# Edge preparation: two of the three weighted key one-hots are multiplied on GpSimd instead of VectorE

## The chip, the cores and the metric

The kernel runs on one core of one Trainium2 chip. The metric is device time of a whole execution in microseconds; the kernel before has a median of 10035.09 us over 3 runs (10032.35 to 10036.63). A core has TensorE (matrix multiply, writes PSUM), VectorE, ScalarE, GpSimd and SyncE (which here only issues DMAs). In rows of the profile they are PE (PEld is its weight load), DVE, ACT, POOL and SP.

## What is computed

Four graph layers run one after the other over 6250 nodes with 128 features and 200,000 edges sorted by target node: a GCN, a typed message layer with a GRU, an attention layer and an MPNN, each added to its input and normalized.

```
x = _layernorm(x + _L0_gnn_ref(x, edge_index, edge_weight, W, b))
x = _layernorm(x + _L1_gnn_ref(x, edge_index, edge_type_8, ...))
x = _layernorm(x + _L2_gnn_ref(x, edge_index, ...))
x = _layernorm(x + _L3_gnn_ref(x, edge_index, edge_attr_64, ...))
```

Each layer gathers a row per edge (by `src`) and sums rows per target (by `dst`). The GCN weighs an edge by `edge_weight`. All layers share the same edges, so the kernel sorts the edges into a table once, before the first layer. That preparation is the part changed here.

## The kernel before

Edges come in 112 groups of 14 x 128 (GC = 14 columns on 128 partitions). An *item* is one group against one window of 128 target nodes; there are 112 items here, handled by a loop of 28 turns with four items each (SL = 4). Every engine runs its own loop over the same items, and semaphores keep them in step.

For an item k the work is this; lines are those of the profile.

- GpSimd *picks*: it copies and shifts the item's slices of the edge fields into small tiles (L681 to L691), among them `w2`, the edge weight split into three bf16 parts, each value doubled. It starts once TensorE has finished the window sums (L958) of item k - 2, since `product` counts those, and signals `posted`.
- VectorE, `key_hot(k)`: the window test and the key (L778, L779), then OJ, the one-hot of each edge's key, 128 x 1372 bf16 (1372 = 14 x 98; L783), and how many edges of the same row have the same key (L785 to L789).
- TensorE, `ranks(k)` (L934 to L939): prefix sums and totals of OJ into PSUM.
- VectorE, `rank_hot(k - 1)`, in the turn after: copies of the prefix sums from PSUM (L804, L805), the product of OJ and the prefix (L808), three folding steps (L810 to L812), an add (L813), the one-hot of the rank OHr (L814) and a maximum (L817).
- ScalarE: two of the five fields of OJF, OJ times a per-edge number (L719), and copies of the edge terms out of PSUM (L708).
- VectorE, `weigh_keys(k)`: the other three fields of OJF, OJ times each part of `w2` (L839, three instructions of 128 x 1372 bf16).
- TensorE, `place(k)` (L949), one turn later: 14 matmuls that place the five fields by OHr; it waits for OHr (`hot_rank`), ScalarE's fields (`scaled`) and VectorE's (`wdone`).
- VectorE, `rec_add(k - 2)`: what was placed is added from PSUM into X and acc (L827, L830).
- VectorE, `window_hot(k)` (L846), and TensorE's window sums from it (L958). TensorE also multiplies the edge attributes in the loop (L969).

So one turn on VectorE is `key_hot(k)`, `rank_hot(k-1)`, `rec_add(k-2)`, `weigh_keys(k)`, `window_hot(k)`, and one on TensorE is half of the edge terms, `ranks(k)`, `place(k-1)`, the other half, window sums of k. OJ, OJF and w2 have two buffers each, by the parity of the item; OJF is 128 x 14 x 5 x 98, so one field of it is 14 pieces of 98 elements that lie 490 apart. Most VectorE instructions wait on the one before through the semaphore `chain` (the helper `own.step`).

Two other places of the program are used below to read prices: the GCN pass, where GpSimd adds the three parts of the weights (L1651, L1653, 128 x 2450) while VectorE subtracts tiles (L1675, 128 x 896 f32).

Of the kernel before, what the change touches and what calls it, by code (L numbers as in the profile page):

```python
# [30 lines left out]
ALU = mybir.AluOpType  # L31
# [17 lines left out]
SL = 4  # L49
# [20 lines left out]
BK = 2 * NT  # L70
# [37 lines left out]
def passed(eng, tick):  # L108

    eng.sem_inc(tick, 1)

def over(ap, n):

    return ap.unsqueeze(2).to_broadcast([ap.shape[0], ap.shape[1], n])
# [7 lines left out]
def build(nc, x, xT, src, dst, edge_type, edge_weight, edge_attr, wpack, mats, rowpack, colpack, out):  # L124
    V = nc.vector
# [37 lines left out]
    def sems(prefix, names):  # L163

        made = [nc.alloc_semaphore(name=f"{prefix}_{n}") for n in names.split()]
        in_stage.extend(made)
        return made
# [8 lines left out]
    with ExitStack() as whole:  # L176
# [372 lines left out]
        with ExitStack() as ctx:  # L549
# [8 lines left out]
            w2 = sb(ctx, "prep_w2", [P, 2, 3, GC, 2], BF16)  # L558
# [12 lines left out]
            OJ = sb(ctx, "prep_OJ", [P, 2, GC, BK], BF16)  # L571
            OJF = sb(ctx, "prep_OJF", [P, 2, GC, 5, BK], BF16)
# [24 lines left out]
            zeroed, posted, hotd, hot_key, scaled, wdone, prefix_ready, prefix_free, hot_rank, place_ready, place_free = sems(  # L597
                "prep", "zeroed posted hotd hot_key scaled wdone prefix_ready prefix_free hot_rank place_ready place_free")
# [2 lines left out]
            totalled, slots_out, begun, taken = sems("prep", "totalled slots_out begun taken")  # L601
            fields_blank, ends_out, cleaned = sems("prep", "fields_blank ends_out cleaned")
            attr_in = sems("prep", "attr_in0 attr_in1")
            terms_out = sems("prep", "terms_out0 terms_out1")
            term_ready, term_taken, terms_done, spares, si_ready = sems("prep", "term_ready term_taken terms_done spares si_ready")
            KEY_STEPS, RANK_STEPS, ADD_STEPS = 6, 8, 2
            STEPS = KEY_STEPS + RANK_STEPS + ADD_STEPS
            with nc.Block() as block:
# [55 lines left out]
                @block.gpsimd  # L664
                def _(pool):
                    nc.gpsimd.memset(OJF[:], 0.0).then_inc(fields_blank, 1)
                    pool.wait_ge(zeroed, 1)
                    n = pool.value_load(turns_to[0:1, NCH:NCH + 1], min_val=1, max_val=KCAP // SL)
                    with pool.Fori(0, n) as i:
                        for s in range(SL):  # L670
                            k, par = i * SL + s, s % 2
                            pool.wait_ge(item_ready[s], i * 16 + 16)
                            passed(pool, tick)
                            g = pool.value_load(itm[0:1, s, 2:3], min_val=0, max_val=NG - 1)
                            pool.wait_ge(hot_key, k + 1)
                            pool.wait_ge(scaled, k + 1)
                            pool.wait_ge(wdone, k + 1)
                            pool.wait_ge(product, k + 1)
                            pool.wait_ge(hotd, k + 1)
                            fg = FLD[:, ds(g, 1)].rearrange("p g f c -> p (g f) c")  # L680
                            nc.gpsimd.tensor_copy(dg[:], dstI[:, ds(g * GC, GC)])  # L681
                            nc.gpsimd.tensor_copy(kg[:], KEY0[:, ds(g * GC, GC)]).then_inc(taken, 1)
                            pool.wait_ge(taken, k + 1)
                            passed(pool, tick)
                            nc.gpsimd.tensor_scalar(off[:, par], dg[:], itm[:, s, 0:1], None, ALU.subtract)
                            nc.gpsimd.tensor_scalar(kk[:, par], kg[:], itm[:, s, 3:4], None, ALU.subtract)
                            nc.gpsimd.tensor_scalar(at[:, par], over(dg[:], 2), itm[:, s, 0:1], None, ALU.subtract)
                            nc.gpsimd.tensor_copy(fld[:, par], fg[:, 0:2, :])
                            nc.gpsimd.tensor_copy(w2[:, par].rearrange("p f c a -> p (f c) a"),
                                                  over(FLD[:, ds(g, 1), 2:5, :].rearrange("p g f c -> p (g f c)"), 2))  # L690
                            nc.gpsimd.tensor_copy(wm[:, par, 0:3], fg[:, 2:5, :]).then_inc(posted, 1)  # L691
                            pool.wait_ge(posted, k + 1)
                            passed(pool, tick)
                    pool.wait_ge(terms_done, 1)
                    pool.iota(spare_rows, [[P, NG * GC]], base=NSLOT, channel_multiplier=1,
                              allow_small_or_imprecise_dtypes=True).then_inc(spares, 1)
# [42 lines left out]
                def _(dve):  # L739
                    own = Chain(dve, begun)  # L740
# [4 lines left out]
                    own.step(V.memset(RK[:], 0.0))  # L745
                    own.step(V.memset(within[:], 0.0))
                    own.step(V.memset(wm[:], 1.0))
                    own.step(V.tensor_copy(iob[:], iota_row[:]))
                    own.step(V.tensor_tensor(out=lower[:], in0=over(iota_row[:, 0:GC], GC), in1=rows(iota_row[:, 0:GC], GC),
                                             op=ALU.is_gt))  # L750
# [6 lines left out]
                    dve.sem_inc(hot_key, 2)  # L757
                    dve.sem_inc(scaled, 2)
                    dve.sem_inc(wdone, 2)
                    dve.sem_inc(hotd, 2)  # L760
                    dve.sem_inc(place_free, 1)
                    dve.wait_ge(fields_blank, 1)

                    def pairs(a2, n):
                        return a2.unsqueeze(2).to_broadcast([P, GC, n // 2, 2])

                    def halves(t):
                        return t.rearrange("p c (h a) -> p c h a", a=2)

                    def same_rows(b, n):  # L770
                        return b.rearrange("p (h a) -> p h a", a=2).unsqueeze(1).to_broadcast([P, GC, n // 2, 2])

                    def key_hot(k, s, own):
                        par = s % 2
                        n0 = own.n
                        dve.wait_ge(posted, k + 1)
                        dve.wait_ge(hot_key, k + 2)
                        own.step(V.tensor_single_scalar(win[:], off[:, par], 7, op=ALU.arith_shift_right))  # L778
                        own.step(V.scalar_tensor_tensor(out=key2[:], in0=over(win[:], 2), scalar=MISS, in1=over(kk[:, par], 2),  # L779
                                                        op0=ALU.mult, op1=ALU.add))  # L780
                        dve.wait_ge(scaled, k + 1)
                        dve.wait_ge(wdone, k + 1)
                        V.tensor_tensor(out=halves(OJ[:, par]), in0=pairs(key2[:], BK), in1=same_rows(iob[:, 0:BK], BK),  # L783
                                        op=ALU.is_equal).then_inc(hot_key, 1)
                        own.step(V.tensor_tensor(out=twin[:], in0=over(key2[:, :, 0], GC), in1=rows(key2[:, :, 0], GC),  # L785
                                                 op=ALU.is_equal))
                        own.step(V.tensor_tensor(out=twin[:], in0=twin[:], in1=lower[:], op=ALU.mult))
                        own.step(V.tensor_reduce(within[:, par], twin[:], AX, ALU.add))
                        own.step(V.scalar_tensor_tensor(out=within[:, par], in0=win[:], scalar=0.0, in1=within[:, par],  # L789
                                                        op0=ALU.is_equal, op1=ALU.mult))  # L790
                        assert own.n - n0 == KEY_STEPS
# [42 lines left out]
                    def weigh_keys(k, s):  # L834
                        par = s % 2
                        dve.wait_ge(hot_key, k + 3)
                        dve.wait_ge(place_ready, k + 1)
                        for a in range(3):
                            ins = V.tensor_tensor(out=halves(OJF[:, par, :, 2 + a, :]), in0=halves(OJ[:, par]),  # L839
                                                  in1=pairs(w2[:, par, a], BK), op=ALU.mult)  # L840
                        ins.then_inc(wdone, 1)

                    def window_hot(k, s):
                        par = s % 2
# [5 lines left out]
                    with dve.Fori(0, n) as i:  # L850
# [3 lines left out]
                        for s in range(SL):  # L854
                            k = i * SL + s
# [69 lines left out]
                def _(pe):  # L925
# [16 lines left out]
                    def place(k, s):  # L942
                        par = s % 2
                        pe.wait_ge(hot_rank, k + 2)
                        pe.wait_ge(scaled, k + 3)
                        pe.wait_ge(wdone, k + 3)
                        pe.wait_ge(place_free, k + 2)
                        for c in range(GC):
                            mm = pe.matmul(placed[par], OHr[:, par, c, :], OJF[:, par, c].rearrange("p f b -> p (f b)"),  # L949
                                           start=c == 0, stop=c == GC - 1)  # L950
                        mm.then_inc(place_ready, 1)
# [2274 lines left out]
```

## Time and profile before

| | |
|---|---|
| median of 3 runs | 10035.09 us |
| the profiled execution | 10033.66 us, span 10031.9 us |
| busy, TensorE matmul / VectorE / ScalarE / GpSimd | 8345.2 / 7403.1 / 3377.0 / 2329.2 us |
| mean granted TensorE clock | 0.883 of full speed |
| edge loop of preparation | about 123 to 1545 us, 14% of the span |
| granted clock in the loop | 0.91 |

The span runs from the first to the last instruction. Shares of busy time over the whole span mix stages with different limits, so the loop is looked at by itself, from the first to the last of the weight multiplies. Two instructions whose times overlap by a few hundredths are pipelined on one engine. An instruction's time in the profile includes any time for which it was issued and could not proceed.

### The profile page before, as it was taken

The numbers are of one execution on the slowest core, as the hardware profiler recorded it, in microseconds if no ns is written. First come the engines' busy times: TensorE is split into PE (matmuls) and PEld (weight loads), VectorE is DVE, ScalarE is ACT, GpSimd is POOL, SyncE is SP. The second block draws the span as 40 slices with busy tenths as digits, with TensorE's granted clock in tenths as the row PEclk, the third lists the DMA queues.
The fourth block names the chain that finished last, engine by engine and source line by source line (L and its number), as shares of the span: only waits on it lengthen the run. The fifth ranks groups of instructions, "written<-read, shape, count | busy, mean of one in ns | idle before, by whom it ended". The sixth has DMA issues, their size and how long they took to land. (4 is left out here: it accounts for less than half of the span.)

```text
span 10031.9 us, 275228 instructions
## 1 busy us (share of the span) xinstructions
PE 8345.2 (83%) x104317; PEld 6699.0 (67%) x104318; DVE 7403.1 (74%) x11896; ACT 3377.0 (34%) x7132; POOL 2329.2 (23%) x3048
## 2 busy tenths in 40 slices
PE   5777772599959999996699999955886999599983
PEld 4545551599946666664466666635886999499982
DVE  7888888888857666664466766635997888788875
ACT  4777771100015444443244444411330000133321
POOL 2111110000014555553155555510331000100010
PEclk8999995799969999998799999976557999699986
DMA  3333331566633333331233333302772222166650
GB/s 97 110 110 110 110 110 43 164 248 248 248 137 132 115 122 118 121 116 60 68 119 119 121 115 122 114 30 80 302 294 88 94 93 92 66 247 248 248 190 11
DMA packets 393197, 1349.67 MB, mean 135 GB/s; under 512 B 111251, under 2 KB 174781, under 8 KB 354621
## 3 DMA queue, kind: packets, MB, share of 16 engines
q1 hardware_dynamic: 261629, 1054.90, 29.5%
q10 hardware_dynamic: 72704, 173.74, 4.6%
q0 software_dynamic: 58688, 118.70, 3.8%
q8 instruction: 109, 1.79, 0.1%
q14 instruction: 67, 0.55, 0.0%
HBM read 940.84 MB, written 406.28 MB: 134 GB/s over the span
## 5 line engine op out<-in xcount | busy, mean ns | idle before, releaser
L2077 PE MATMUL typed_GP<-typed_hd,typed_Gb 128*128 128x256 bf16 x15288 | 1942.5, 274 | 0.0
L2012 ACT CAST typed_Gb<-typed_GP 128x768 bf16<-128x768 f32 (+1 forms) x1568 | 1336.5, 852 | 1276.0 <-PE typed_GP L2058 635.6
L2077 PEld LDWEIGHTS typed_GP<-typed_hd,typed_Gb 128*128 128x128 bf16 x15288 | 1366.9, 98 | 555.2 <-issue 250.9
L1919 POOL DMA_INDIRECT es_d<-X x1568 | 1574.9, 1004 | 525.1 <-issue 476.7
L1964 DVE TENSOR_TENSOR typed_hd<-typed_recv,typed_iota2b 128x768 bf16<-128x768 bf16 (+1 forms) x1568 | 929.6, 593 | 642.2 <-PE typed_GP L2077 642.0
L1974 DVE CAST typed_Gb<-typed_GP 128x384 bf16<-128x384 f32 (+1 forms) x1568 | 925.1, 590 | 322.5 <-PE typed_GP L2062 166.5
L2058 PE MATMUL typed_GP<-typed_H,typed_hsT 128*32 128x384 bf16 x18816 | 1054.8, 330 | 66.7 <-ACT typed_H L2005 66.7
L719 ACT ACTIVATE prep_OJF<-prep_OJ,prep_fld 128x98 bf16<-128x98 bf16 x3136 | 861.9, 368 | 123.3 <-DVE prep_OJ L783 123.1
L2058 PEld LDWEIGHTS typed_GP<-typed_H,typed_hsT 128*32 128x32 bf16 x18816 | 357.6, 95 | 523.6 <-issue 237.9
L949 PE MATMUL prep_PS<-prep_OJF,prep_OHr 128*128 128x490 bf16 x1582 | 466.7, 461 | 234.2 <-DVE prep_OHr L814 234.2
L1806 PE MATMUL mpnn_GP<-mpnn_hd,mpnn_et 128*128 128x128 f32 x4802 | 578.7, 277 | 2.4 <-issue 1.4
L1806 PE MATMUL gcn_GP<-gcn_hd,gcn_msg 128*128 128x128 f32 x4802 | 578.6, 277 | 0.0
L1806 PE MATMUL heads_GP<-heads_hd,heads_msg 128*128 128x128 f32 x4802 | 578.5, 277 | 0.0
L1806 PEld LDWEIGHTS mpnn_GP<-mpnn_hd,mpnn_et 128*128 128x128 f32 x4802 | 551.6, 192 | 2.7 <-issue 2.7
L1806 PEld LDWEIGHTS gcn_GP<-gcn_hd,gcn_msg 128*128 128x128 f32 x4802 | 551.7, 192 | 0.0
L1806 PEld LDWEIGHTS heads_GP<-heads_hd,heads_msg 128*128 128x128 f32 x4802 | 551.6, 192 | 0.0
L1758 ACT ACTIVATE mpnn_et<-mpnn_et 128x1536 f32<-128x1536 f32 x196 | 296.1, 1511 | 646.9 <-DVE mpnn_et L1709 646.9
L1958 DVE TENSOR_SCALAR typed_hsT<-typed_rows,iota_col 128x384 bf16<-128x384 bf16 (+1 forms) x1568 | 508.6, 324 | 0.0
L949 PEld LDWEIGHTS prep_PS<-prep_OJF,prep_OHr 128*128 128x128 bf16 x1582 | 175.3, 116 | 482.4 <-issue 217.4
L1791 PE MATMUL gcn_GP<-gcn_H,gcn_hsT 128*128 128x128 bf16 x7203 | 437.2, 220 | 37.0 <-ACT gcn_H L1750 27.6
L1693 DVE TENSOR_TENSOR mpnn_hd<-recD,iota 128x1536 f32<-128x1536 f32 (+1 forms) x196 | 351.1, 1792 | 154.8 <-PE mpnn_GP L1806 154.8
L1693 DVE TENSOR_TENSOR heads_hd<-recD,iota 128x1536 f32<-128x1536 f32 (+1 forms) x196 | 351.1, 1791 | 153.5 <-PE heads_GP L1806 153.5
(576 smaller groups left out, 13893.1 us busy)
## 6 DMA issues: line engine op xcount, KB each, us to landing
typed_rows<-slott_d SPq DMA_DIRECT2D x196, 832.0 KB, 4.2
HB<-slot_d SPq DMA_DIRECT2D x98, 1568.0 KB
es_d<-gcn_blank ACTq DMA_DIRECT2D x49, 3136.0 KB, 10.1
ba_rows<-slot_d SPq DMA_DIRECT2D x49, 3136.0 KB
mpnn_et<-es_d SPq DMA_DIRECT2D x147, 768.0 KB, 4.2
X<-et_d SPq DMA_DIRECT2D x98, 1024.0 KB
heads_rows<-slot_d SPq DMA_DIRECT2D x49, 1568.0 KB
et_d<-wt_early SPq DMA_DIRECT2D x112, 512.0 KB, 2.6
```

What stands on the lines that cost most here:

```text
L719: ins = act.activation(OJF[:, par, c, f, :], OJ[:, par, c, :], ACT.Copy, scale=fld[:, par, f, c:c + 1])
L949: mm = pe.matmul(placed[par], OHr[:, par, c, :], OJF[:, par, c].rearrange("p f b -> p (f b)"), start=c == 0, stop=c == GC - 1)
L1693: V.tensor_tensor(out=hd[:, par, 0:nb], in0=over(recd[:, ds(n * (2 * NT) + (ip * NT + at), nb)], P), in1=rows(iota1[:], nb), op=ALU.is_equ ...
L1791: mm = pe.matmul(odd if b == 12 else gp[par][:, b], hsT[:, par, b, :], H3[:, a, j * P:(j + 1) * P], start=a == 0, stop=a == 2)
L1806: mm = pe.matmul(accp, et[:, u, b, :] if edge_own else msg[:, par, b, :], hd[:, par, b, :], start=j == 0, stop=j == NT - 1)
L1919: pool.indirect_dma_start(es_d, bass.IndirectOffsetOnAxis(ap=SI[:, at:at + 1], axis=0), ET[:, i % 2, c, :], None).then_inc(scattered[i % 2 ...
L1958: V.tensor_scalar(hsT[:, v % 2, 0:n].rearrange("p b n -> p (b n)"), rowsb[:, h, o:o + n * P], iota1_col[:, 0:1], None, ALU.is_equal).then_ ...
L1964: V.tensor_tensor(out=hd[:, v % 2, 0:n].rearrange("p b (h a) -> p b h a", a=2), in0=recv2[:, ds(i * QC + q, n)].unsqueeze(2).to_broadcast( ...
L1974: V.tensor_copy(Gb[:, par, 2, 0:w], GP[:, 3 * par + 2, 0:w]).then_inc(evD, 1)
L2012: act.copy(Gb[:, par, 0:2, 0:w], GP[:, 3 * par:3 * par + 2, 0:w]).then_inc(evA, 1)
L2058: mm = pe.matmul(GP[to, 3 * par + ch, 0:3 * P], hot, H3[:, j].rearrange("p a f -> p (a f)"), start=True, stop=True)
L2077: mm = pe.matmul(agg(a), gathered(par, ch, k), hd[:, par, ch, :], start=q0 == 0 and ch == 0 and k == 0, stop=False, skip_group_check=True)
```

## The change

In `weigh_keys` VectorE keeps the first of the three multiplies. The two others are done by GpSimd, in a function `weigh_rest(k - 1, s - 1)` that is called behind the picks of item k. A semaphore `wrest` counts them: TensorE's `place` waits for it, VectorE waits for it before it writes OJ of item k over that of k - 2, and GpSimd waits for it before its picks. The call of the first turn multiplies blank weights (w2 is set to zero before the loop), and one call follows behind the loop, for the last item. The GpSimd multiply reads one value of each doubled pair of `w2`, repeated over the 98 keys.

```diff
+                    def weigh_rest(k, s):
+                        par = s % 2
+                        pool.wait_ge(hot_key, k + 3)
+                        for a in range(1, 3):
+                            ins = nc.gpsimd.tensor_tensor(out=OJF[:, par, :, 2 + a, :], in0=OJ[:, par], in1=over(w2[:, par, a, :, 0], BK),
+                                                          op=ALU.mult)
+                        ins.then_inc(wrest, 1)
...
                             pool.wait_ge(wdone, k + 1)
+                            pool.wait_ge(wrest, k + 1)
...
                             pool.wait_ge(posted, k + 1)
                             passed(pool, tick)
+                            weigh_rest(k - 1, s - 1)
+                    pool.wait_ge(place_ready, n * SL)
+                    weigh_rest(n * SL - 1, SL - 1)
...
+                    own.step(V.memset(w2[:], 0.0))
...
+                    dve.sem_inc(wrest, 1)
...
                         dve.wait_ge(wdone, k + 1)
+                        dve.wait_ge(wrest, k + 1)
...
-                        for a in range(3):
-                            ins = V.tensor_tensor(out=halves(OJF[:, par, :, 2 + a, :]), in0=halves(OJ[:, par]),
-                                                  in1=pairs(w2[:, par, a], BK), op=ALU.mult)
-                        ins.then_inc(wdone, 1)
+                        V.tensor_tensor(out=halves(OJF[:, par, :, 2, :]), in0=halves(OJ[:, par]),
+                                        in1=pairs(w2[:, par, 0], BK), op=ALU.mult).then_inc(wdone, 1)
...
                         pe.wait_ge(wdone, k + 3)
+                        pe.wait_ge(wrest, k + 3)
```

On VectorE, at the end of an item, the program before has these rows (line, operation, output<-inputs, shape; "L105" is the wait of `own.step`):

```order
L827 TENSOR_TENSOR X<-X,prep_PS 128x5x98
L105 REGISTER_ALU
L830 ISA
L830 TENSOR_TENSOR acc<-acc,prep_PS 4x128
L105 REGISTER_ALU
L836 REGISTER_ALU
L839 TENSOR_TENSOR prep_OJF<-prep_OJ,prep_w 128x14x98 x3
L846 TENSOR_TENSOR prep_OHd<-prep_at,prep_iob 128x1792
```

And the changed program at the same place of VectorE (line numbers are some 15 higher):

```order
L843 TENSOR_TENSOR X<-X,prep_PS 128x5x98
L105 REGISTER_ALU
L846 ISA
L846 TENSOR_TENSOR acc<-acc,prep_PS 4x128
L105 REGISTER_ALU
L852 REGISTER_ALU
L854 TENSOR_TENSOR prep_OJF<-prep_OJ,prep_w 128x14x98
L860 TENSOR_TENSOR prep_OHd<-prep_at,prep_iob 128x1792
```

One multiply stands where three stood; nothing else moves on VectorE.

On GpSimd, from the end of one item's picks to the start of the next, before:

```order
L688 COPY prep_fld<-FLD 128x28
L689 ISA
L689 COPY prep_w<-FLD 128x84
L691 COPY prep_wm<-FLD 128x42
L674 TENSOR_LOAD prep_itm
L674 ISA x2
L675 REGISTER_ALU
L681 ISA
L681 COPY prep_dg<-dstI 128x14
```

And in the changed program:

```order
L698 COPY prep_fld<-FLD 128x28
L699 ISA
L699 COPY prep_w<-FLD 128x84
L701 COPY prep_wm<-FLD 128x42
L672 REGISTER_ALU
L674 TENSOR_TENSOR prep_OJF<-prep_OJ,prep_w 128x14x98 x2
L683 TENSOR_LOAD prep_itm
L683 ISA x2
L691 ISA
L691 COPY prep_dg<-dstI 128x14
```

The two multiplies stand between the picks of an item and those of the next one.

## Rows read from the trace of the kernel before

**Rows 1.** Edge loop: length, busy us of PE, PEld, DVE, ACT, POOL; clock, DMA.
```profile
135.00:1532.00 1397.00, 1078.73 (x7997) 701.54 (x7995) 1212.50 (x2446) 1039.46 (x3555) 259.99 (x880) 0.91 0.30 109
```

**Rows 2.** Waits in the same stretch: who, for whom, total us, times, longest.
```profile
POOL prep_dg L681 <- PE prep_PS L958: 811.1, 76, 12.9
...
PE prep_PS L949 <- DVE prep_OHr L814: 229.7, 111, 2.4
...
PE prep_PS L934 <- DVEq L806: 53.7, 62, 1.7
```

**Rows 3.** The window one-hot, L846: ns min/median/max, first and last start.
```profile
L846 DVE TENSOR_TENSOR prep_OHd<-prep_at,prep_iob x112: 1081/1085/1086, 137.4 to 1531.9; 128x1792 bf16<-128x1792 bf16 x112
```

**Rows 4.** VectorE in order of time over one item (start us, us, line, operation).
```profile
804.48 0.17 DVE L778 TENSOR_SCALAR prep_win<-prep_off 128x14 int32<-128x14 int32 x1
...
816.66 0.17 DVE L778 TENSOR_SCALAR prep_win<-prep_off 128x14 int32<-128x14 int32 x1
...
819.38 0.26 DVE L804 TENSOR_SCALAR prep_cnt<-prep_PS 128x98 f32 x1
...
820.09 0.88 DVE L808 TENSOR_TENSOR prep_prod<-prep_OJ,prep_pfx 128x1372 bf16<-128x1372 bf16 x1 [0.15 <-DVE prep_pfx L805]
...
821.99 0.53 DVE L812 TENSOR_REDUCE prep_rank<-prep_prod 128x14 f32<-128x364 bf16 x1
...
822.77 1.09 DVE L814 TENSOR_TENSOR prep_OHr<-prep_rank,prep_iob 128x1792 bf16<-128x1792 bf16 x1
823.78 0.17 DVE L817 TENSOR_TENSOR prep_RK<-prep_RK,prep_rank 128x14 bf16 x1
824.07 0.67 DVE L827 TENSOR_TENSOR X<-X,prep_PS 128x490 f32 x1
824.99 0.28 DVE L830 TENSOR_TENSOR acc<-acc,prep_PS 4x128 f32 x1 [0.25 <-DVE X L827]
825.57 2.44 DVE L839 TENSOR_TENSOR prep_OJF<-prep_OJ,prep_w 128x1372 bf16<-128x1372 bf16 x3 [0.30 <-DVE acc L830]
```

**Rows 5.** The weight multiplies in the loop (count, busy us, mean ns).
```profile
L839 DVE TENSOR_TENSOR prep_OJF<-prep_OJ,prep_w 128x1372 bf16<-128x1372 bf16 x336 | 273.4, 869 | 37.8 <-DVE acc L830 37.8
```

**Rows 6.** GpSimd in order of time, edge weights of the gcn pass.
```profile
1842.80 4.28 POOL L1651 TENSOR_TENSOR gcn_recw<-X 128x2450 f32<-128x2450 bf16 x1
1847.15 5.55 POOL L1653 TENSOR_TENSOR gcn_recw<-gcn_recw,X 128x2450 f32<-128x2450 f32 x1
```

**Rows 7.** VectorE's L1675 there: ns min/median/max, then its two delayed instructions.
```profile
L1675 DVE TENSOR_TENSOR acc<-HB,gcn_H x7: 1077/1077/5703, 1843.2 to 1857.6; 128x896 f32<-128x896 f32 x7
...
1843.21 4.81 DVE L1675 TENSOR_TENSOR acc<-HB,gcn_H 128x896 f32<-128x896 f32 x1
...
1847.94 5.70 DVE L1675 TENSOR_TENSOR acc<-HB,gcn_H 128x896 f32<-128x896 f32 x1
```

**Rows 8.** GpSimd in order of time over two items of the loop.
```profile
805.91 0.20 POOL L681 COPY prep_dg<-dstI 128x14 int32 x1 [8.33 <-DVE prep_OJ L783]
...
807.69 0.22 POOL L691 COPY prep_wm<-FLD 128x42 bf16 x1
818.85 0.20 POOL L681 COPY prep_dg<-dstI 128x14 int32 x1 [10.94 <-PE prep_PS L958]
...
820.05 1.06 POOL L687 TENSOR_SCALAR prep_at<-prep_dg,prep_itm 128x28 bf16<-128x28 int32 x1
...
821.71 0.31 POOL L691 COPY prep_wm<-FLD 128x42 bf16 x1
```

**Rows 9.** A pick on GpSimd and a folding add on VectorE: ns min/median/max.
```profile
L687 POOL TENSOR_SCALAR prep_at<-prep_dg,prep_itm x112: 350/362/1072, 124.7 to 1511.9; 128x28 bf16<-128x28 int32 x112
...
L811 DVE TENSOR_TENSOR prep_prod<-prep_prod x113: 334/336/409, 130.6 to 1536.2; 128x336 bf16<-128x336 bf16 x113
```

**Rows 10.** TensorE in order of time: placing, and the window sums behind it.
```profile
811.67 4.66 PE L949 MATMUL prep_PS<-prep_OJF,prep_OHr 128*128 128x490 bf16 x14 [2.10 <-DVE prep_OHr L814]
...
817.55 0.95 PE L958 MATMUL prep_PS<-prep_OHd,prep_wm 128*4 128x128 bf16 x14
```

More of the change, by code:

```diff
@@ L603, in build @@
             attr_in = sems("prep", "attr_in0 attr_in1")
+            wrest, = sems("prep", "wrest")
             terms_out = sems("prep", "terms_out0 terms_out1")
```

## Prediction

> **What bounds the kernel now.** I began with the busy time by engine over the loop that prepares the edges [rows 1]: between 135 and 1532 us VectorE is busy 1212.5 of 1397 us (87%), TensorE 1078.7, ScalarE 1039.5, GpSimd only 260.0. Then I read the waits of that stretch [rows 2]. The large ones are waits of the others: TensorE waits 229.7 us for VectorE's rank one-hot (prep_OHr) and 53.7 us for VectorE to free the prefix sums, GpSimd 811.1 us for TensorE. No wait of VectorE on another engine is among them. So VectorE sets the pace here. The loop has 112 items; its last instruction of an item starts first at 137.4 and last at 1531.9 us [rows 3], so an item takes (1531.9 - 137.4) / 111 = 12.56 us.
>
> Next I laid out one item on VectorE [rows 4]. Counted from the start of L778, the product with the prefix (L808) starts at 3.43 us and takes 0.88, the rank one-hot (L814) starts at 6.11, the maximum into RK (L817) at 7.12, the addition into X (L827) at 7.41, and the three weight multiplies (L839) at 8.91, for 2.44; the window one-hot (L846, 1.08 [rows 3]) closes the item. Between L808 and L814 stand the folding adds L810 and L811, the reduce L812 and a small add. What matters below: the adds into X and acc (L827, L830) and the two copies of the prefix sums (L804, L805) take an operand from PSUM (prep_PS), the reduces L788 and L812 and the shift L778 have one input, and nearly all the rest is tensor_tensor with two SBUF inputs.
>
> **What goes.** Two of three L839 multiplies. The group is 336 instructions, 273.4 us busy [rows 5], 2.44 us an item, so 2/3 of it is 1.63 us an item and 112 x 1.63 = 182 us. TensorE would let it through: its waits for VectorE are 229.7 + 53.7 = 283 us [rows 2], 2.53 us an item, more than the 1.63.
>
> **What comes on GpSimd.** Two multiplies an item of 128 x 1372 bf16: 113 pairs, one of them on blank weights in the first turn, the last behind the loop. No row has a two-input multiply of this shape on GpSimd. The nearest are the two adds of edge weights over 2450 columns [rows 6]. L1651, bf16 inputs, had the engine's memory path to itself and took 4.28 us: 1.745 ns a column. L1653, f32, shows 5.55 us, but VectorE's L1675 was in front of it until about 1848.02 (1847.08 + 0.94), which leaves 4.68 us: 1.91 ns a column. For 1372 columns that is 2.39 to 2.62 us; I take 2.5, nearer the bf16 row. As a pair 5.0 us. The upper end, if the whole 5.55 us were its own (2.26 ns), is 3.1 us each.
>
> GpSimd has the room. It is idle for 10.94 us before its picks [rows 8], and 260.0 / 112 = 2.3 us an item busy. The results are wanted late: picks start behind TensorE's L958 of an item k and are for item k + 2; the multiplies behind them are for item k + 1, whose keys VectorE has just made, and which TensorE places only after VectorE's rank step of the next turn, about one item later. So the new waits on wrest (VectorE's before it overwrites OJ, TensorE's before placing) should show nothing, and the extra blanking of w2 is one instruction at the start.
>
> **What it costs VectorE.** This is the step that decides. At 1843 us VectorE's L1675 is a tensor_tensor of two SBUF inputs, and takes 1.077 us in the median [rows 7]. The one that starts at 1843.21, inside GpSimd's L1651, takes 4.81 us, to 1848.02: it finishes 0.94 us after L1651 ended at 1847.08. The next starts at 1847.94, takes 5.70 us, and ends 0.94 us after L1653 ended at 1852.70 [rows 6, 7]. So a VectorE instruction with two SBUF inputs stands still as long as a GpSimd instruction of this kind runs, and the two take turns, one instruction each. Those were f32. In the loop itself, with bf16, it shows in small: GpSimd's pick L687 takes 362 ns in the median but 1072 at most [rows 9], and the one of 1.06 us at 820.05 lies over VectorE's bf16 L808 of 0.88 us [rows 4, 8]; VectorE's L811 goes from 336 ns to 409 at most; a pick has 14 to 84 columns.
>
> Where in the item the pair falls follows from GpSimd's start, which is the end of TensorE's L958. In one pattern L958 follows the window one-hot directly, and the picks run 805.91 to 807.91 [rows 8], where that item's L778 started at 804.48: they end 3.43 us into the item, as L808 starts. Then the first multiply stops L810 for about 2.5 us, L810 runs, and the second stops L811 for 2.5 us: 5.0 us lost, none hidden. L814 and with it the placing (L949) then come late, and TensorE's chain from the start of L949 to the end of L958, 811.67 to 818.50 or 6.8 us [rows 10], ends after the window one-hot: with 3.5 us for the next picks (818.50 to 822.02 [rows 8]) they end 10.3 us after the end of L814, the window one-hot 12.34 - 1.63 - 7.20 = 3.5 us after it, so 6.8 us into the next item, shortly before L817. There the first multiply stops L817 for 2.5 us, the second runs beside L827 and L830, the 1.5 us from 7.41 to 8.91 that take PSUM operands, and stops the remaining L839 for 1.0 us: 3.5 us. The two patterns push each other to alternate; the mean is about 4.2 us an item.
>
> Sum: 4.2 - 1.63 = 2.57 us more an item, x 112 = 288 us, on the profiled execution's 10033.7 us: 10,322. That execution is 1.4 us under the median of the runs (10035.1), so **10,323 us, slower by 2.9%**.
>
> Bounds of the term. Below: all of VectorE's work that needs no second SBUF operand hides under the pair, namely L778, L804, L805 (as L804), L812, L788 (a smaller reduce, at most L812's), L827 and L830, 0.17 + 0.26 + 0.26 + 0.53 + 0.53 + 0.67 + 0.28 = 2.70 us [rows 4], and a multiply costs 2.39: 4.78 - 2.70 = 2.08 us stalled, +0.45 an item, +50 us, 10,085. Above: 3.1 us each and nothing hidden, 6.2 - 1.63 = 4.6 us an item, +512 us, 10,545. If 2.62 and nothing hidden, 3.6 us, +404, 10,438.
>
> The page "GPSIMD Engine Reference" of the Trainium skill, section "Performance versus the Vector engine", gives 4497 ns for 2048 f32 columns of a two-input add, 2.2 ns a column, so as an estimate 3.0 us each and 10,435 by the same sum. L1651's 1.745 ns is lower, and I go by the row.
>
> **Rivals.** (a) Nothing is locked in this pairing, because VectorE's bf16 multiplies run in another mode than L1675's f32. Then VectorE is shorter by 1.63 us an item, TensorE's 2.53 us of waits allow it, and the time is 10,035 - 182 = 9,853. For it: GpSimd stands idle most of each item, and the delay of VectorE's bf16 work that rows 9 show is 73 ns. Against it: the pick that lay over L808 shows that bf16 work does hold GpSimd off, and a lock that works one way only would be odd. It turns at 1.63 us of stall an item: under that the change gains. Chance 0.07.
>
> The mode bears on this: "Advanced Engine Details and Errata" of the Trainium skill, section "VectorE Performance Modes", names only two-port modes as blocking GpSimd, and lists 2x bf16 as using one port; its "GPSIMD Details" adds instructions with two SBUF inputs. The first alone gives rival (a), the second the forecast. L1675 in rows 7, f32 with two inputs, was blocked, so the trace goes with the second there.
>
> (b) The lock holds but most of the pair hides under VectorE's PSUM and one-input work: 10,085 to 10,190. It needs the multiplies to fall on L827 every time, and on reduces or copies besides; the item's layout has at most 1.5 us of such work in a row. Chance 0.13.
>
> (c) The multiply is slower on GpSimd than the long adds, since its rows are of 98 columns, one operand is repeated along each and the output is written in strides: 10,440 to 10,545. No row has that form. Chance 0.15.
>
> **How the numbers follow.** The forecast (3.0 to 5.2 us stalled an item: +1.4 to +3.6 us, 10,190 to 10,440) has 0.65. The range leaves out (a), the lowest of (b) and the upper half of (c): 10,150 to 10,480. Differences under 0.2%, 20 us, can't be told from none in a measurement of this kernel. Faster is (a) less 0.01 for a gain that another wait takes back, 0.06; same is that 0.01 and as much of (b) near its point of no change, 0.02; slower is the rest, 0.92.
>
> **What would show it.** In the profile after: about 224 GpSimd multiplies into OJF at 2.4 to 3.4 us with their waits; single instructions of L811, L817 or the window one-hot near 3 us, against medians of 0.34 and 1.08 for the first and last [rows 3, 9] and 0.17 for L817; an item of about 15 us; TensorE waiting more for L814, and no wait on wrest. I am wrong if L810, L811 and L817 keep their lengths, or if the item gets shorter.

## The result, and the profile after

The changed kernel takes 10286.94 us (median of 4 runs, 10284.35 to 10296.99), the one before 10035.36 us on the same chip: a ratio of 1.0253, 95% interval [1.0235, 1.0271]. The forecast was 10,323 us, 36 us above what came.

The engines' line of the page after (busy us, share of the span, instructions):

```profile
PE 8400.6 (82%) x104317; PEld 6746.9 (66%) x104318; DVE 7628.4 (74%) x11673; ACT 3370.9 (33%) x7132; POOL 2940.8 (29%) x3274
```

VectorE, which issues 224 multiplies less, is busy 225.3 us longer than before (7403.1), and GpSimd 611.6 us longer (2329.2). The loop, by the same view as [rows 1], from the first to the last window one-hot (us; busy of PE, PEld, DVE, ACT, POOL; granted clock; DMA):

```profile
143.00:1786.00 1643.00, 1132.28 (x8002) 750.02 (x8001) 1431.05 (x2222) 1034.65 (x3552) 860.63 (x1102) 0.84 0.26 93
```

VectorE is still the busy one: 1431 of 1643 us, 87% as before. The window one-hot, now L860, by the view of [rows 3] (ns min/median/max, first and last start):

```profile
L860 DVE TENSOR_TENSOR prep_OHd<-prep_at,prep_iob x112: 1076/1084/3367, 143.7 to 1784.5; 128x1792 bf16<-128x1792 bf16 x112
```

(1784.5 - 143.7) / 111 = 14.78 us an item, against 12.56. Most instances keep their 1084 ns; some took up to 3367. VectorE in order of time, as [rows 4] (start us, us, line), over the rank step of one item, and 18 us later the end of the next:

```profile
813.41 0.96 DVE L824 TENSOR_TENSOR prep_prod<-prep_OJ,prep_pfx 128x1372 bf16<-128x1372 bf16 x1 [0.15 <-DVE prep_pfx L821]
814.41 0.51 DVE L826 TENSOR_TENSOR prep_prod<-prep_prod 128x672 bf16<-128x672 bf16 x1
814.95 2.49 DVE L827 TENSOR_TENSOR prep_prod<-prep_prod 128x336 bf16<-128x336 bf16 x1
817.47 0.53 DVE L828 TENSOR_REDUCE prep_rank<-prep_prod 128x14 f32<-128x364 bf16 x1
818.04 1.78 DVE L829 TENSOR_TENSOR prep_rank<-prep_rank,prep_within 128x28 bf16<-128x28 f32 x1
819.85 1.09 DVE L830 TENSOR_TENSOR prep_OHr<-prep_rank,prep_iob 128x1792 bf16<-128x1792 bf16 x1
...
831.94 2.44 DVE L833 TENSOR_TENSOR prep_RK<-prep_RK,prep_rank 128x14 bf16 x1
834.50 0.67 DVE L843 TENSOR_TENSOR X<-X,prep_PS 128x490 f32 x1
...
836.00 1.52 DVE L854 TENSOR_TENSOR prep_OJF<-prep_OJ,prep_w 128x1372 bf16<-128x1372 bf16 x1 [0.30 <-DVE acc L846]
```

And GpSimd's new multiply: ns min/median/max, and the two pairs that belong to those two stretches:

```profile
L674 POOL TENSOR_TENSOR prep_OJF<-prep_OJ,prep_w x226: 2472/2565/3197, 125.9 to 1776.0; 128x1372 bf16<-128x1372 bf16 x113
...
814.70 5.08 POOL L674 TENSOR_TENSOR prep_OJF<-prep_OJ,prep_w 128x1372 bf16<-128x1372 bf16 x2 [0.25 <-POOL prep_wm L701]
...
831.17 5.62 POOL L674 TENSOR_TENSOR prep_OJF<-prep_OJ,prep_w 128x1372 bf16<-128x1372 bf16 x2 [0.34 <-POOL prep_wm L701]
```

These are the two patterns of the prediction. In the first, the pair runs from 814.70 to 819.78: L827 (L811 before, 0.34 us [rows 9]) takes 2.49, and the small add L829 (before: L813, 0.19 at least) takes 1.78 and ends as the pair does, while the reduce L828 between them, with one input, keeps its 0.53. VectorE loses 2.15 + 1.59 = 3.74 us. In the second, the pair runs from 831.17 to 836.79: L833 (before: L817, 0.17) takes 2.44, L843 with its operand from PSUM keeps its 0.67, and the one remaining weight multiply takes 1.52 instead of 0.87. The loss is 2.27 + 0.65 = 2.92 us.

Counted over all items in VectorE's timeline, with "stopped" for an instance that takes more than 1 us above the shortest of its line (counts are mine, from those rows):

```
stopped, of some 113 each: L805 19, L824 19, L826 23, L827 35, L829 15, L833 38, L854 17 (38 more by 0.3 to 1 us), L860 17, L830 3, L801 1, L803 1
never: L793, L794, L799, L804, L820, L821, L828, L843, L846
```

So the place of the pair wanders more than two patterns would have it. What met multiplies and was never stopped is the reduces with one input (L804 and L828, 19 and 15 times) and what reads PSUM (L820, L821, L843, L846, 19 to 55 times). L793 and L794 met none, and L799 one, just after it had started; of these three the counts say nothing. Three rows of waits (who, for whom: us, times, longest) for [rows 2]:

```profile
PE prep_PS L964 <- DVE prep_OHr L830: 307.6, 96, 6.4
...
DVE prep_win L793 <- issue: 57.4, 74, 2.4
...
POOL prep_dg L691 <- POOL prep_OJF L674: 0.4, 1, 0.4
```

TensorE waits 307.6 us for the rank one-hot instead of 229.7. Of a wait on GpSimd's multiplies there is one row, 0.4 us in all. The granted clock in the loop is 0.84 instead of 0.91, and TensorE's matmuls there are busy 1132.3 instead of 1078.7 us; the sums below need no term for that.

### The profile page after: what moved, and what is told of

The parts are those of the page before. It is cut to its first block and busy times, and to the rows that moved or that the text cites. A ratio compares the mean times of both kernels' runs of the same rounds, so it can differ in the third digit from the quotient of the medians.

```text
span 10286.8 us, 275515 instructions
## 1 busy us (share of the span) xinstructions
PE 8400.6 (82%) x104317; PEld 6746.9 (66%) x104318; DVE 7628.4 (74%) x11673; ACT 3370.9 (33%) x7132; POOL 2940.8 (29%) x3274
## 5 line engine op out<-in xcount | busy, mean ns | idle before, releaser
L964 PE MATMUL prep_PS<-prep_OJF,prep_OHr 128*128 128x490 bf16 x1582 | 462.1, 458 | 308.2 <-DVE prep_OHr L830 307.6
L674 POOL TENSOR_TENSOR prep_OJF<-prep_OJ,prep_w 128x1372 bf16<-128x1372 bf16 x226 | 608.2, 2711 | 38.6 <-POOL prep_wm L701 30.6
```

The lines of the kernel that those rows point to most:

```text
L674: ins = nc.gpsimd.tensor_tensor(out=OJF[:, par, :, 2 + a, :], in0=OJ[:, par], in1=over(w2[:, par, a, :, 0], BK), op=ALU.mult)
```

## The experiments

Each is timed against the kernel before on its own chip, where that took 10,035 to 10,043 us.

**The multiplies left out.** Only the first of VectorE's three remains, and nobody does the others.

```diff
-for a in range(3):
-    ins = V.tensor_tensor(out=OJF[.., 2 + a], in0=OJ, in1=w2[.., a]); ins.then_inc(wdone, 1)
+V.tensor_tensor(out=OJF[.., 2], in0=OJ, in1=w2[.., 0]).then_inc(wdone, 1)
```

> The kernel before without the second and third weight multiply: VectorE does only the first, nobody does the others (the two lower parts of the edge weights stay blank in the table, so the GCN weights lack them). Both theories: VectorE's turn is 1.63 us shorter, 112 x 1.63 = 182 us, and TensorE's 2.53 us of waits an item let it through: 9,853 us, 9,850 to 9,880. If TensorE or ScalarE take over as the bound, the gain is less than 120 us, above 9,915. This gives the base against which the multiplies on GpSimd are counted.

Measured: 9939.29 us (9935.30 to 9942.08), ratio 0.9905 [0.9888, 0.9921]. A miss: 95 us are gained, not 182. The page's engines:

```profile
PE 8327.3 (84%) x104317; PEld 6700.3 (67%) x104318; DVE 7236.9 (73%) x11672; ACT 3372.3 (34%) x7132; POOL 2356.1 (24%) x3048
```

VectorE is busy 166.2 us less than before, so the work did go. The recorded alternative for so small a gain, TensorE or ScalarE taking over, is not what the rows show: in the loop VectorE waits for TensorE once, for 4.8 us, and never for ScalarE. But it stands idle more. Its row of waits before L778, an item's first instruction ("issue": nothing that the profile shows is waited for), in the kernel before:

```profile
DVE prep_win L778 <- issue: 31.2, 27, 1.2
```

and here:

```profile
DVE prep_win L778 <- issue: 100.5, 111, 2.7
```

69.3 us of idle time came in where the multiplies went: 166.2 - 69.3 = 96.9, against a measured 95.4. In time order, the head of a loop turn and two items inside one (idle time in brackets):

```profile
781.33 0.18 DVE L778 TENSOR_SCALAR prep_win<-prep_off 128x14 int32<-128x14 int32 x1 [2.65 <-issue]
...
803.41 0.17 DVE L778 TENSOR_SCALAR prep_win<-prep_off 128x14 int32<-128x14 int32 x1 [0.21 <-issue]
...
814.44 0.17 DVE L778 TENSOR_SCALAR prep_win<-prep_off 128x14 int32<-128x14 int32 x1 [0.33 <-issue]
```

In the program, VectorE's queue stands there on loads of table values into registers: three for an item, six and the loop's branch at the head of a turn. The loads run in VectorE's instruction stream behind the issue of the window one-hot. With three multiplies queued ahead, most of their time would be covered. At the head of a turn the median gap is 1.15 us in the kernel before and 2.65 here (my count from the timelines): 1.50 more, where 2.44 - 0.87 = 1.57 us of multiplies went. That the loads make it is a reading, which the next run tests.

**The same, with one load less at the head of a turn.** It leaves out what the kernel above leaves out, and one of the six loads besides.

```diff
-last = places(SL - 2)         # loads three values of the last item but one
+last = places_last(SL - 2)    # two: the third is not used
```

> The kernel with the two multiplies left out, with one of the six value loads at the head of VectorE's loop turn taken away (the group number of the item before last, which nothing there uses). That kernel gained 95 us where 182 were expected. Theory: VectorE's own sequencer is busy with the value loads between the window one-hot and the next window test, once an item, and with six of them and the loop's branch once a turn; the multiplies used to cover it, and 100.5 us of idle time before L778 are exposed (2.65 us at the head of a turn, 0.2 to 0.3 else). Then one load less shortens the gap of 2.65 us by about 0.6, 28 x 0.6 = 17 us: 9,915 to 9,930. Rival: VectorE waits there for another engine (GpSimd's picks or the item's DMA): the gap stays 2.65 us, 9,935 to 9,945.

Measured: 9915.59 us (9913.36 to 9921.96), ratio 0.988 [0.9865, 0.9895], so 23.7 us under the one above. The idle time before L778:

```profile
DVE prep_win L778 <- issue: 84.4, 111, 2.1
```

One load of six, 28 times, takes 16.1 us from it, and 0.6 us from the longest. In the profiled executions, 21.3 us apart, 4.1 us more went from the idle time before the one remaining weight multiply (37.8 to 33.7 us); why, no run shows. That a load counts in the gap before L778 is shown, against the rival that VectorE waits there for another engine; that the 84.4 us left are loads too is argued from it.
**The multiplies beside the old kernel.** VectorE keeps its three; GpSimd runs two of the same form on tiles of its own, for which no other engine waits.

```diff
+for a in range(2):    # behind the picks; side_in, side_w, side_out are GpSimd's own
+    nc.gpsimd.tensor_tensor(out=side_out, in0=side_in, in1=over(side_w[:, a], BK), op=ALU.mult)
```

> The kernel before, all three multiplies on VectorE; GpSimd does two extra multiplies of 128 x 1372 bf16 behind each item's picks, from a tile of its own into a tile of its own. No other engine waits for them or uses them. Port theory (VectorE stands still while GpSimd reads two operands from SBUF): an item grows by what it lost in the changed kernel, 14.78 - (12.56 - 1.63) = 3.85 us, 112 x 3.85 = 431 us: about 10,465, 10,400 to 10,500. Wait theory (the changed kernel lost its time on the results of GpSimd, that is on wrest and on picks that start later): nobody waits here, so 10,035, at most 10,060.

Measured: 10487.85 us (10474.12 to 10488.52), ratio 1.0447 [1.0430, 1.0465]: +453 us, with no result of GpSimd's to wait for. The GpSimd multiply, VectorE's maximum into RK (ns min/median/max), and the page's engines:

```profile
L701 POOL TENSOR_TENSOR prep_side_out<-prep_side_in,prep_side_w x224: 2472/2618/3424, 127.8 to 1961.7; 128x1372 bf16<-128x1372 bf16 x112
...
L831 DVE TENSOR_TENSOR prep_RK<-prep_RK,prep_rank x113: 164/2436/2448, 138.8 to 1989.1; 128x14 bf16 x113
...
PE 8435.1 (80%) x104317; PEld 6740.2 (64%) x104318; DVE 7860.6 (75%) x11898; ACT 3374.8 (32%) x7132; POOL 2974.0 (28%) x3272
```

The maximum, 0.17 us by itself, takes 2.44 in the median of its 113: one whole GpSimd multiply. VectorE is busy 457.5 us longer than before, and that is the 453 us. Rival (a), no lock between these two, is out, and so is a wait on new semaphores as the cause.

**A GpSimd that only writes.** The same places, but two fills of 2976 bf16 columns, which read nothing.

```diff
+for a in range(2): nc.gpsimd.memset(side_out, 0.0)    # 128 x 2976
```

> As the kernel with extra multiplies beside, but with two memsets of 2976 bf16 columns instead, each about 2.5 us long by the memset of OJF (11.53 us for 13720 columns): GpSimd is busy as long, but reads nothing from SBUF. If it is GpSimd's reading that stops VectorE's two-input instructions: 10,035 to 10,070. If any busy GpSimd does (its writes, or the engine as such): 10,400 to 10,500. Wait theory: 10,035.

Measured: 10035.81 us, ratio 1.0001 [0.9992, 1.0011]. The fills, and the maximum into RK:

```profile
L700 POOL MEMSET prep_side_out<- x224: 2577/2578/2579, 126.8 to 1517.8; 128x2976 bf16 x112
...
L827 DVE TENSOR_TENSOR prep_RK<-prep_RK,prep_rank x113: 165/166/169, 133.3 to 1541.2; 128x14 bf16 x113
```

and GpSimd and VectorE in one stretch of time:

```profile
824.75 2.58 POOL L700 MEMSET prep_side_out<- 128x2976 bf16 x1 [0.41 <-POOL prep_wm L694]
...
825.24 0.19 DVE L823 TENSOR_TENSOR prep_rank<-prep_rank,prep_within 128x28 bf16<-128x28 f32 x1
825.46 1.09 DVE L824 TENSOR_TENSOR prep_OHr<-prep_rank,prep_iob 128x1792 bf16<-128x1792 bf16 x1
826.47 0.17 DVE L827 TENSOR_TENSOR prep_RK<-prep_RK,prep_rank 128x14 bf16 x1
```

Three two-input instructions of VectorE run at full speed inside one fill of 2.58 us. A busy GpSimd and its writes cost nothing that can be measured here; what the multiplies have beyond them is the reading of SBUF and the arithmetic, and the copies below tell the two apart. The Trainium skill names the reading, in "SBUF — State Buffer", section "SBUF: two separate sides": a VectorE instruction with two SBUF inputs takes an exclusive lock only against a GpSimd one that reads SBUF, and who starts first holds it for the whole instruction. This run and the one above agree with both halves.

**A GpSimd that copies.** As the multiplies beside the old kernel, with copies of the same size, one input each.

```diff
-    nc.gpsimd.tensor_tensor(out=side_out, in0=side_in, in1=over(side_w[:, a], BK), op=ALU.mult)
+    nc.gpsimd.tensor_copy(side_out, side_in)
```

> As the kernel with extra multiplies beside, but with two copies of the 1372 bf16 columns (one input instead of two). If GpSimd's reading takes the port whatever the number of inputs, the loss goes with the copies' length: at 0.95 ns a column (a cast of 1568 columns took 1.50 us) 1.3 us each, half the multiplies': 0.5 x 453 = +230 us, 10,200 to 10,300. If only GpSimd's second input stands in VectorE's way: 10,035 to 10,060.

Measured: 10251.46 us (10247.98 to 10251.75), ratio 1.0213 [1.0197, 1.0228]: +215 us.

```profile
L702 POOL COPY prep_side_out<-prep_side_in x224: 1330/1376/2181, 127.6 to 1729.5; 128x1372 bf16<-128x1372 bf16 x112
...
PE 8420.6 (82%) x104317; PEld 6718.6 (66%) x104318; DVE 7621.5 (74%) x11898; ACT 3375.4 (33%) x7132; POOL 2712.2 (26%) x3272
```

VectorE is busy 218.4 us longer. GpSimd's own time is 224 x 1.330 = 298 us here and 224 x 2.472 = 554 us with the multiplies; 73% and 83% of it landed on VectorE. So in instructions of 1.3 us and more the price goes roughly by GpSimd's time with SBUF reads; one input is enough for it, and no arithmetic is needed.

**One multiply instead of two.** GpSimd does the third part only, VectorE the first two.

```diff
-for a in range(1, 3):    # GpSimd
+for a in range(2, 3):
```

> The changed kernel with only the third part on GpSimd; VectorE does two multiplies. Port theory: half of each term, 0.81 us saved and about 1.9 us stalled an item, +1.1 x 112 = +125 us: 10,160, 10,110 to 10,210. Wait theory: GpSimd's result comes 2.6 us sooner, the wait on it goes, and the kernel gains on before: 9,945 to 10,035.

Measured: 10207.26 us (10206.45 to 10214.58), ratio 1.0174 [1.0157, 1.0191]: slower by 173 us, 47 more than the value I had named and inside its range only at the upper end. GpSimd's multiply, ns min/median/max:

```profile
L674 POOL TENSOR_TENSOR prep_OJF<-prep_OJ,prep_w x113: 2479/2863/3281, 126.0 to 1695.0; 128x1372 bf16<-128x1372 bf16 x113
```

Half of the move brings 172.5 of 251.6 us, 69% of the loss: moving a second multiply costs less than moving the first. The expectation took the same share for both. Counted as above, the 113 single multiplies stop a VectorE instruction for over 1 us 113 times (L833, the maximum into RK, 41 times), and the 226 of the changed kernel 188 times, with 38 smaller delays.

**The multiplies cut in four.** The changed kernel, each GpSimd multiply as pieces of 3, 4, 3 and 4 of the 14 columns.

```diff
-ins = nc.gpsimd.tensor_tensor(out=OJF[.., 2 + a], in0=OJ, ...)
+for c0, c1 in ((0, 3), (3, 7), (7, 10), (10, 14)):
+    ins = nc.gpsimd.tensor_tensor(out=OJF[.., c0:c1, 2 + a], in0=OJ[.., c0:c1], ...)
```

> The changed kernel with each GpSimd multiply cut into four instructions (3, 4, 3 and 4 of the 14 pieces), eight short ones instead of two long. If the columns that GpSimd reads are what costs (the port is taken for the data, whatever the length of an instruction): as the changed kernel, 10,270 to 10,340, with eight VectorE instructions an item that wait 0.5 to 0.7 us each instead of two that wait up to 2.5. If what costs is that a short VectorE instruction waits out a long one, and short ones slip into its gaps: clearly less, 10,100 to 10,200.

Measured: 10181.89 us (10179.07 to 10184.26), ratio 1.0139 [1.0123, 1.0154]. Of the two expectations the second holds: the same columns cost VectorE less when they come in short instructions. Against the kernel with the multiplies left out, the loss falls from 347 us (251.6 + 95.4) to 234 (139.0 + 95.4). VectorE in time order, and the eight GpSimd pieces that lie over it:

```profile
820.64 0.86 DVE L827 TENSOR_TENSOR prep_prod<-prep_prod 128x672 bf16<-128x672 bf16 x1
821.53 0.85 DVE L828 TENSOR_TENSOR prep_prod<-prep_prod 128x336 bf16<-128x336 bf16 x1
822.42 0.53 DVE L829 TENSOR_REDUCE prep_rank<-prep_prod 128x14 f32<-128x364 bf16 x1
822.99 0.77 DVE L830 TENSOR_TENSOR prep_rank<-prep_rank,prep_within 128x28 bf16<-128x28 f32 x1
823.79 1.50 DVE L831 TENSOR_TENSOR prep_OHr<-prep_rank,prep_iob 128x1792 bf16<-128x1792 bf16 x1
825.22 0.81 DVE L834 TENSOR_TENSOR prep_RK<-prep_RK,prep_rank 128x14 bf16 x1
826.15 0.67 DVE L844 TENSOR_TENSOR X<-X,prep_PS 128x490 f32 x1
...
819.86 7.58 POOL L675 TENSOR_TENSOR prep_OJF<-prep_OJ,prep_w 128x294 bf16<-128x294 bf16 x8 [0.25 <-POOL prep_wm L702]
```

Each two-input instruction is late by 0.35 to 0.65 us (L834 takes 0.81, not 0.17) instead of one or two by 2.2, while L829 and L844 go free. The page's engines:

```profile
PE 8361.4 (82%) x104317; PEld 6709.7 (66%) x104318; DVE 7508.9 (74%) x11673; ACT 3374.2 (33%) x7132; POOL 3216.0 (32%) x3952
```

VectorE is busy 119.5 us less than in the changed kernel, GpSimd 275.2 us more. The 904 pieces of 0.67 us at least are 606 us of GpSimd's own time, of which 272 (7508.9 - 7236.9), 45%, landed on VectorE. That shorter turns let more of GpSimd's time pass beside VectorE's other work fits these rows, but no run separates it from the fixed part of an instruction: left open.

These pieces also meet an instruction that the pairs never met, the shift at the head of an item (now L794, L793 in the changed kernel). It has one input, and input and output lie in SBUF:

```profile
L794 DVE TENSOR_SCALAR prep_win<-prep_off x112: 163/176/810, 126.2 to 1655.6; 128x14 int32<-128x14 int32 x112
...
429.04 1.52 POOL L675 TENSOR_TENSOR prep_OJF<-prep_OJ,prep_w 128x294 bf16<-128x294 bf16 x1
...
429.95 0.64 DVE L794 TENSOR_SCALAR prep_win<-prep_off 128x14 int32<-128x14 int32 x1
```

Of its 112 instances 52 meet a piece; they take 0.34 to 0.81 us and each ends 0.03 us behind the piece (430.59 and 430.56 above), and no other takes over 0.18. So a second SBUF input is not the only thing that makes a VectorE instruction wait.

**Small instructions instead of large ones.** GpSimd makes the window test and the key (L778, L779 on VectorE before) within its picks, from tiles of 14 to 28 columns; the multiplies are all VectorE's.

```diff
-own.step(V.tensor_single_scalar(win, off, 7, op=arith_shift_right))
-own.step(V.scalar_tensor_tensor(out=key2, in0=win, scalar=MISS, in1=kk, op0=mult, op1=add))
+nc.gpsimd.tensor_scalar(off, dg, itm, MISS, subtract, mult)
+nc.gpsimd.tensor_scalar(wins, off, 0.0, (P - 1) * MISS, max, min)
+nc.gpsimd.tensor_tensor(out=wins, in0=wins, in1=off, op=subtract)
+nc.gpsimd.tensor_tensor(out=keys, in0=wins, in1=kk, op=add)
```

> The kernel before (all three weight multiplies on VectorE), with another piece of work moved to GpSimd: the window test and the key of 14 and 28 columns (VectorE's L778 and L779, 0.43 us of its turn) are made in the picks by three small GpSimd instructions. Port theory: their 14 to 28 columns hold VectorE for under 0.1 us each, while VectorE loses 0.43 us of fixed cost an item: -0.43 + 0.1 to 0.2, so -25 to -40 us, 9,990 to 10,010. If GpSimd instructions cost VectorE by their count or length in the profile (0.3 us each): 10,035 to 10,100. If the picks now end too late for the next item's key: above 10,035.

Measured: 9993.03 us (9992.54 to 9997.06), ratio 0.9952 [0.9939, 0.9966]. The two GpSimd instructions with two inputs (busy us, mean ns):

```profile
L701 POOL TENSOR_TENSOR prep_keys<-prep_wins,prep_kk 128x28 bf16<-128x28 f32 x110 | 52.0, 472 | 0.0
...
L695 POOL TENSOR_TENSOR prep_wins<-prep_wins,prep_off 128x14 f32<-128x14 f32 x110 | 32.6, 297 | 4.0
```

They take 0.47 and 0.30 us, and VectorE's busy time falls to 7365.5 us, by 37.6. Here work went from VectorE to GpSimd at a gain.

**That, with one load less.** The complete kernel, with both edits.

> The kernel with the small key instructions on GpSimd (0.5% under before), with the same value load taken away. Its gap at the head of a turn is 1.4 us at most; one load less takes some 0.6 us of it in each of 28 turns: -17 us, 9,970 to 9,985. By the rival (another engine is waited for) no change, 9,990 to 10,000.

Measured: 9970.70 us (median of 5 runs, 9967.56 to 9976.25), ratio 0.9934 [0.9920, 0.9947]. It computes everything, and at 0.66% under the kernel before it is the fastest such version here. Each against its own kernel before, it gains 65.4 us, and the one above 49.9. The idle time before the item's first VectorE instruction (now L792) without the load removed:

```profile
DVE prep_OJ L792 <- issue: 33.8, 27, 1.4
```

and with it removed:

```profile
DVE prep_OJ L792 <- issue: 17.4, 27, 0.7
```

16.4 us over 27 turns is 0.6 us a load, the size that the left-out multiplies gave.

## Why the prediction was right, and where it wasn't

The sign, the mechanism and the range held; two terms of the sum were mis-sized, in opposite directions, and the closeness of the total, 10,323 against 10,287, owes something to that.

- *VectorE sets the pace.* Right. What it gains or loses in busy time is the kernel's time, once idle time before L778 is counted: from the left-out kernel to the changed one VectorE gains 7628.4 - 7236.9 = 391.5 us, of which 100.5 - 57.4 = 43.1 fill that idle time. 348.4 us remain, and 347.0 were measured. GpSimd's own time was 226 x 2.472 = 559 us; 70% of it (391.5) landed on VectorE.
- *What goes: 1.63 us an item, 182 us.* Mis-sized. It is 95.4 us, 0.85 an item. Of 182 us of multiplies VectorE's busy time loses only 166.2: a single one takes 0.87 us, where three in a row, which overlap, take 2.44, so 1.57 us an item or 176 us go, and most of the rest is L778, which no longer overlaps the window one-hot before it. And 69.3 come back as idle time before L778, where the register loads stand that the multiplies had covered. The prediction named TensorE as what could be late next, and not VectorE's own instruction stream.
- *A GpSimd multiply takes 2.39 to 2.62 us.* Right: 2.472 at least, 1.80 ns a column; pairs of 5.08 and 5.62 us with their turns. Rival (c), a slower multiply, is out.
- *VectorE stands still for two SBUF inputs.* Right, and now for bf16 (0.34 to 2.49 us); rival (a) is out. The converse is not right throughout: the lower bound lets the shift L778 (0.17 of its 2.70 us) run beside a multiply, and in the kernel cut in four the same shift was held.
- *Two patterns, 5.0 and 3.5 us, mean 4.2.* Right in kind, too dear in size. The first costs 3.74, since the pair started one instruction later, so that L811 and not L810 was stopped, and the reduce ran free between the two stops. The second costs 2.92: L817 lost 2.27 and the multiply 0.65, for 2.5 and 1.0. There are other places too (L805, L824, L860). Over all items VectorE's instructions are longer by 391.5 / 112 = 3.50 us; 43.1 us of that, 0.38 an item, cost nothing, as they fall into the idle time. So 3.1 us stand for 4.2. Rival (b), 10,085 to 10,190, stands for 2.1 to 3.0 us by the prediction's sum; the stall, 3.1 to 3.5 us, came out just above that, so (b) missed by little there, and the time lies outside its range also because the gain was smaller.
- *The sum.* 3.1 - 0.85 = 2.25 us an item, 252 us, where 4.2 - 1.63 = 2.57 was forecast, 288.
- *What would show it.* Single L811 (now L827) and L817 (L833) near 2.5 us, the window one-hot at up to 3.37, an item of 14.78 us, a longer wait for L814 (L830), no wait of note on the new semaphore: all there. 226 multiplies, where "about 224" stood.

## What to carry to other kernels

Before work goes from VectorE to an idle GpSimd, list what VectorE runs meanwhile: of GpSimd's time in SBUF-reading instructions of 1.3 to 2.5 us, 70 to 83% came back here as VectorE time, since most of VectorE's work has two SBUF inputs, and 45% in pieces of 0.7 us. Small instructions (0.3 to 0.5 us) went over at a gain, and fills, which only write, cost nothing beside VectorE. And before time is taken off the bounding engine, look at the idle time before the first instruction behind it: idle time where register loads stand in its own queue ate 69 of 166 us, and one load dropped at the head of a turn gave 16 us of them back.

## What was not expected of the hardware

- GpSimd fills of 2.58 us beside VectorE's two-input instructions, 224 of them: +1 us in the whole kernel, which can't be told from none.
- One-input copies on GpSimd (1.33 us) stop VectorE just as two-input multiplies do: 73% of their time.
- A VectorE shift with one input, SBUF to SBUF, is held by a GpSimd multiply too (0.17 us to 0.81), while reduces and what reads PSUM run beside one.
- Eight short GpSimd instructions an item cost VectorE less than two long ones of the same columns, 234 against 347 us, though GpSimd itself is busy longer.
- A value load in VectorE's stream at the head of a turn costs 0.6 us, with 0.9 us of multiplies queued before it (16.1 us in all) as with 2.4 us (16.4 us). Before the items inside a turn, with three loads each, 0.2 to 0.8 us of idle time show with 0.9 us of multiplies, and none with 2.4 us.
